# Cross attention with its scores made twice, and the experts' work placed in the next batches' steps

## The reference

```python
# cross attention: channels are attended, 8 heads of 32 tokens each; keys and values are the context
qk = einsum('bhdq,bhdl->bhql', qh, kh) / sqrt(32)      # q: x, k = v: ctx, 512 x 512 per head
ret = einsum('bhql,bhdl->bhdq', softmax(qk), vh)
x = layernorm(x + gamma * ret)
# experts: 8 of rank 16, two per token
gates = softmax(x @ Wr + br + bonus); w = two largest gates, divided by their sum
x = layernorm(x + sum_e w_e * (relu(x @ Wd_e + bd_e) @ Wu_e + bu_e))
```

## Time and profile before

| | |
|---|---|
| median of 3 runs | 2082.64 us |
| the profiled execution, its own time | 2083.66 us |
| its span (first to last instruction) | 2081.9 us |
| TensorE busy, share of the span | 1846.4 us, 89% |
| VectorE | 1249.2 us, 60% |
| ScalarE | 920.4 us, 44% |
| GpSimd | 288.0 us, 14% |
| mean granted TensorE clock | 0.952 |

### The profile page before, as it was taken

How to read it: one execution, slowest core, us unless ns; L and a number is a source line. 1 busy time by engine, 2 the same in 40 slices (tenths; PEclk the granted TensorE clock), 3 DMA queues, 4 the chain that set the end, 5 groups by cost and what they waited for, 6 DMA issues and landing times. The chain is left out here.

```text
span 2081.9 us, 33021 instructions
## 1 busy us (share of the span) xinstructions
PE 1846.4 (89%) x12272; PEld 1503.4 (72%) x12272; DVE 1249.2 (60%) x2330; ACT 920.4 (44%) x2376; POOL 288.0 (14%) x347
## 2 busy tenths in 40 slices
PE   6979999999976799999999996799997498889966
PEld 5868999998964588888888985677775365555543
DVE  3446444444434565546555536788887288878847
ACT  2224333333323343333333223666666288878811
POOL 0000000000002111111111001333343111121001
PEclk9989999999997799999999998999998699999988
DMA  3122000000013231111101013000010675556234
GB/s 104 45 97 72 21 21 21 21 21 21 10 48 101 66 97 47 36 31 41 46 19 34 11 41 121 11 31 32 31 42 21 182 179 136 153 140 149 68 114 142
DMA packets 86253, 136.62 MB, mean 66 GB/s; under 512 B 9480, under 2 KB 25480, under 8 KB 86096
## 3 DMA queue, kind: packets, MB, share of 16 engines
q1 hardware_dynamic: 86096, 134.52, 22.3%
HBM read 79.88 MB, written 21.05 MB: 48 GB/s over the span
## 5 line engine op out<-in xcount | busy, mean ns | idle before, releaser
L1164 PE MATMUL yp<-ccy,toep 128*128 128x288 f32 x640 | 182.4, 436 | 19.5 <-POOL ccy L892 13.4
L1965 ACT ACTIVATE e_p<-e_s_ps,e_nb 128x512 f32<-128x512 f32 x256 | 175.0, 696 | 51.6 <-DVE e_nb L2013 49.5
L2013 DVE TENSOR_REDUCE e_nb<-e_s_ps 128x2 f32<-128x1024 f32 x128 | 155.8, 1218 | 54.3 <-PE e_s_ps L2090 53.5
L1442 ACT ACTIVATE p<-p,nb,rq 128x128 f32<-128x128 f32 (+1 forms) x256 | 137.0, 541 | 94.5 <-DVE nb L1539 94.5
L2100 PE MATMUL e_t_ps<-ident,e_p 128*128 128x128 f32 x1024 | 148.7, 284 | 24.7 <-DVE e_pT L2020 13.2
L1164 PEld LDWEIGHTS yp<-ccy,toep 128*128 128x128 f32 x640 | 126.5, 206 | 55.7 <-POOL ccy L892 14.8
L2100 PEld LDWEIGHTS e_t_ps<-ident,e_p 128*128 128x128 f32 x1024 | 120.8, 146 | 62.5 <-issue 52.9
L80 PE MATMUL q_ps<-a_xt_hi,wq_hi 128*128 128x256 f32 x512 | 151.7, 296 | 4.1 <-DVE wo_lo L112 4.1
L1062 DVE SCALAR_TENSOR_TENSOR hm<-gu_ps,us_col,sg 128x256 f32<-128x256 f32 x88 | 42.3, 481 | 182.3 <-ACT sg L971 182.3
L82 PE MATMUL q_ps<-a_xt_hi,wq_lo 128*128 128x256 f32 x512 | 146.5, 286 | 0.0
L81 PE MATMUL q_ps<-a_xt_lo,wq_hi 128*128 128x256 f32 x512 | 146.4, 286 | 0.0
(11 more groups left out here) (277 smaller groups left out, 5122.1 us busy)
## 6 DMA issues: line engine op xcount, KB each, us to landing
x_after<-n_r SPq DMA_DIRECT2D x24, 512.0 KB, 3.0
toep<-padded_kernels SPq DMA_DIRECT2D x32, 256.0 KB, 3.5
qs<-e_xh SPq DMA_DIRECT2D x64, 128.0 KB, 2.5
qs<-e_xl SPq DMA_DIRECT2D x64, 128.0 KB, 2.6
ks<-e_ch SPq DMA_DIRECT2D x64, 128.0 KB, 2.6
ks<-e_cl SPq DMA_DIRECT2D x64, 128.0 KB, 2.6
x<-x_after SPq DMA_DIRECT2D x12, 512.0 KB, 4.7
x<-in_x SPq DMA_DIRECT2D x8, 512.0 KB, 4.1
```

The lines of the kernel that those rows point to most:

```text
L1164: last = pe.matmul(yp[:, lo % 2, 0:NCOL], toep[h % 2][:, (lo - li) * P:(lo - li + 1) * P], ccy[h % 2][:, li, 0:NCOL], start=(li == 0), sto ...
L1442: act.activation(p[n % 3][:, h, part[t]], p[n % 3][:, h, part[t]], ACT.Exp, bias=nb[i][:, t, h:h + 1], scale=rq[u][:, t:t + 1], accum_out= ...
L1965: act.activation(pr[i][:, a, :], s_ps[i][:, a, :], ACT.Exp, bias=nb[i][:, a:a + 1], accum_out=sums[t][:, j, q:q + 1]).then_inc(e_done, 1)
L2013: dve.tensor_reduce(nb[i][:], s_ps[i][:], AX.X, ALU.max, negate=True).then_inc(nb_done, 1)
```

## The change

One function, `l1_cross_and_experts`, takes the place of both.

- **Scores twice.** "Rough" scores (`rough_scores`) are one matmul of 32 rows per head and query block, from the rounded high parts alone, two heads at once in different rows of the array. They are made for the maxima only, and run 11 steps ahead (`LEAD`). VectorE writes the negated maxima (`maxima`, still 128x1024 per step) into `nbx`; a transposition (`turn_largest`, four tiles, twice a batch) and a ScalarE copy turn them into rows; four DMAs issued by ScalarE (`place_largest`) put them into row 96 of `qs`, whose partner row of `ks` holds ones. The exact scores (`scores`) have keys on partitions and 97 rows: three stacked parts and the maximum. So ScalarE's exponentials go from PSUM straight to `pT`, with no bias and no sum, and the transpositions and their copies fall away. SyncE stacks with 24 DMAs per batch in place of 32.
- **Sums.** `values` has four more matmuls that multiply by `ones`, so the sums lie in `d_ps` spread over partitions already. `normalise` takes the reciprocal of all 128x512 of them, and scales. `v_ps` and `d_ps` are single: the first values of a tile wait for the `normalise` of the tile before (`o_scaled`). GpSimd adds the residual.
- **Experts.** Their operations stand in the cross attention's steps of the next two batches, at fixed steps of each engine's order. x stays on chip; the experts' loads of x and the store and reload of the tensor between are gone.
- **PSUM.** Rough scores, context, turned maxima, x, hidden, turned and out all share `a_ps`, two slots of two banks each, strictly in turn. `take` makes TensorE wait until the reader of the use before last is done.

The diff, cut to its core (`+` and `-` where the line is new or gone; indices as in the order of the steps):

```diff
-STEPS = HX * NQ // 2
-HALF = STEPS // 2
-
-
-def l1_cross(core, ahead, after, x, ctx_in, y, gamma):
+STEPS = T * NQ * HT // 2
+UNITS = 2 * STEPS
+LEAD = 11
+NPT = 12
+KX = 3 * CX + 1
...
+def l1_cross_and_experts(core, ahead, x, ctx_in, y, gamma, wr, br, wdn, bd, wup, bu):
...
+        nbx = [sb(f"e_nbx{i}", [P, NQ, P]) for i in range(2)]
+        nbr = [sb(f"e_nbr{i}", [P, D], F32R) for i in range(2)]
+        pT = [sb(f"e_pT{i}", [P, D]) for i in range(NPT)]
+        ones = sb("e_ones", [P, CX])
+        rec = sb("e_rec", [P, D])
+        rb = [sb(f"e_rb{i}", [P, D]) for i in range(2)]
...
+        a_ps = [pb(f"e_a_ps{i}", [P, 2, D]) for i in range(2)]
+        s_ps = [pb(f"e_s_ps{i}", [P, D]) for i in range(2)]
+        v_ps, d_ps = pb("e_v_ps", [P, D]), pb("e_d_ps", [P, D])
...
+        def slot_uses(b, step, g):
+
+            if step == 1 and 0 <= b - 2 < B:
+                yield "out", b - 2
+            if step == 3 and 0 < b + 1 < B:
+                yield "context", b + 1
+            if step in (5, 13) and 0 <= 2 * b + 1 + step // 8 < 2 * B:
+                yield "largest", 2 * b + 1 + step // 8
+            if step == 8 and 0 <= b - 1 < B:
+                yield "x", b - 1
+            if step == 10 and 0 <= b - 1 < B:
+                yield "hidden", b - 1
+            if step == 15 and 0 <= b - 1 < B:
+                yield "turned", b - 1
+            if 0 <= g + LEAD < PAIRS_IN_ALL:
+                yield "pair", g + LEAD
+
+        place = {("context", 0): 0}
+        for at in steps():
+            for use in slot_uses(*at):
+                place[use] = len(place)
...
+                for b, step, g in steps():
+                    if step == 3 and 0 <= b - 2 < B:
+                        power(b - 2, mv6, mv6_done, y6_done, rstd6, ve6_done, rstd6_done)
+                    if step == 3 and 0 <= b - 1 < B:
+                        residual(b - 1, 1)
+                    if step == 6 and 0 <= b - 1 < B:
+                        power(b - 1, mv5, mv5_done, y5_done, rstd5, ve5_done, rstd5_done)
+                    if step == 6 and b + 2 < B:
+                        scale_x(b + 2)
+                    if step == 10 and b + 2 < B:
+                        take_lo(pool, b + 2, "cl")
+                    if step == 11 and 0 <= b < B:
+                        residual(b, 0)
+                    if step == 12 and b + 2 < B:
+                        take_lo(pool, b + 2, "xl")
...
+                def place_largest(n):
+
+                    b, t = divmod(n, T)
+                    act.wait_ge(nbr_done, n + 1)
+                    if b >= 2:
+                        act.wait_ge(s_mm, UNITS * (b - 2) + UNITS // 2 * (t + 1))
+                    for j in range(HT):
+                        act.dma_start(qs[b % 2][KX - 1:KX, t, j, :].bitcast(F32),
+                                      nbr[n % 2][j * CX:j * CX + 1, :].bitcast(F32)).then_inc(biased, 16)
+
+                def exps(u):
+                    act.wait_ge(s_mm, u + 1)
+                    if u >= NPT:
+                        act.wait_ge(pv_mm, (u - NPT) // HT + 1)
+                    act.activation(pT[u % NPT][:], s_ps[u % 2][:], ACT.Exp).then_inc(e_done, 1)
...
+                for b, step, g in steps():
+                    if step == 1 and 0 <= b - 2 < B:
+                        hidden(b - 2)
+                    if step in (6, 14) and 0 <= 2 * b + 1 + step // 8 < 2 * B:
+                        place_largest(2 * b + 1 + step // 8)
+                    if 0 <= g < PAIRS_IN_ALL:
+                        exps(2 * g)
+                        exps(2 * g + 1)
+                    if step == 4 and 0 < b + 1 < B:
+                        context(b + 1)
+                    if step in (5, 13) and 0 <= 2 * b + 1 + step // 8 < 2 * B:
+                        round_largest(2 * b + 1 + step // 8)
+                    if step == 9 and 0 <= b - 1 < B:
+                        turned(b - 1)
+                    if step == 9 and b + 2 < B:
+                        round_hi(b + 2, "ch")
+                    if step == 11 and b + 2 < B:
+                        round_hi(b + 2, "xh")
+                    if step == 12 and 0 <= b - 1 < B:
+                        exponential(b - 1)
...
+                def maxima(n):
+                    b, t, q, jj = pair(n)
+                    half = n // (STEPS // 2)
+                    dve.wait_ge(a_mm, n + 1)
+                    if half >= 2:
+                        dve.wait_ge(n_turned, half - 1)
+                    heads = nbx[half % 2][:, q, :].rearrange("p (j c) -> p j c", c=CX)[:, 2 * jj:2 * jj + 2, 0]
+                    dve.tensor_reduce(heads, slot("pair", n)[:], AX.X, ALU.max, negate=True).then_inc(nb_done, 1)
+
+                def normalise(n):
+                    dve.wait_ge(pv_mm, NQ * (n + 1))
+                    if n:
+                        dve.wait_ge(o_scaled, n)
+                    dve.reciprocal(rec[:], d_ps[:]).then_inc(rec_done, 1)
+                    dve.wait_ge(rec_done, n + 1)
+                    if n >= 2:
+                        dve.wait_ge(added5, n - 1)
+                    dve.scalar_tensor_tensor(rb[n % 2][:], v_ps[:], gcol[:, 0:1], rec[:], ALU.mult, ALU.mult)\
+                       .then_inc(o_scaled, 1)
...
+                def add_experts(b):
+                    dve.wait_ge(o_mm, b + 1)
+                    dve.tensor_tensor(rr[b % 2][:], slot("out", b)[:], rr[b % 2][:], ALU.add).then_inc(added6, 1)
...
+                for u in range(2):
+                    dve.memset(ks[u][KX - 1:KX, :, :, :].bitcast(F32), 1.0).then_inc(set_up, 1)
+                take_lo(dve, 0, "cl")
+                take_lo(dve, 0, "xl")
+                dve.wait_ge(set_up, 5)
+                dve.wait_ge(g_loaded, 16)
+                for b, step, g in steps():
+                    if step == 2 and 0 <= b - 2 < B:
+                        add_experts(b - 2)
+                    if step == 11 and 0 <= b - 1 < B:
+                        shift(b - 1)
+                    if 0 <= g + LEAD < PAIRS_IN_ALL:
+                        maxima(g + LEAD)
+                    if b == 0 and step == 0:
+                        dve.wait_ge(w_loaded, 64)
+                        dve.tensor_scalar(bias[:, 0, 0:E], bias[:, 0, 0:E], BONUS, None, ALU.add).then_inc(prepared, 1)
+                        dve.wait_ge(prepared, 3)
+                    if step in (2, 10) and 0 <= 2 * b - 1 + step // 8 < 2 * B:
+                        normalise(2 * b - 1 + step // 8)
+                    if step == 2 and 0 <= b - 2 < B:
+                        statistics(b - 2, added6, b - 1, st6, st6_done, mv6, mv6_done)
+                    if step == 4 and 0 <= b - 2 < B:
+                        apply(b - 2, mv6, rstd6, rstd6_done, y6_done)
+                    if step == 5 and 0 <= b - 1 < B:
+                        statistics(b - 1, added5, T * b, st5, st5_done, mv5, mv5_done)
+                    if step == 7 and 0 <= b - 1 < B:
+                        apply(b - 1, mv5, rstd5, rstd5_done, y5_done)
+                    if step == 13 and 0 <= b - 1 < B:
+                        gate(b - 1)
+                        choose(b - 1)
+                    if step == 14 and 0 <= b - 1 < B:
+                        picks(b - 1)
+                        weigh(b - 1)
 
...
+                def take(kind, n, *freed):
+
+                    i = place[kind, n] % 2
+                    if read[i]:
+                        pe.wait_ge(*read[i])
+                    read[i] = freed
+                    return a_ps[i]
...
+                def rough_scores(n):
+
+                    b, t, q, jj = pair(n)
+                    if t == q == jj == 0:
+                        pe.wait_ge(xh_done, b + 1)
+                        pe.wait_ge(ch_done, b + 1)
+                    bank = take("pair", n, nb_done, n + 1)
+                    for i in range(2):
+                        j = 2 * jj + i
+                        d = slice(j * CX, (j + 1) * CX)
+                        last = pe.matmul(bank[:, i, :], xh[b % 2][d, t, q * P:(q + 1) * P], ch[b % 2][d, t, :],
+                                         start=True, stop=True, skip_group_check=True, tile_position=(j * CX, 0))
+                    last.then_inc(a_mm, 1)
+
+                def turn_largest(n):
+                    pe.wait_ge(nb_done, STEPS // 2 * (n + 1))
+                    bank = take("largest", n, nbr_done, n + 1)
+                    for q in range(NQ):
+                        last = pe.transpose(bank[:, 0, q * P:(q + 1) * P], nbx[n % 2][:, q, :], core.ident[:])
+                    last.then_inc(n_turned, 1)
+
+                def scores(u):
+                    b, t, k, j = unit(u)
+                    if k == 0:
+                        pe.wait_ge(stacked[j], 16 * 6 * (b + 1))
+                        pe.wait_ge(biased, 16 * HT * (T * b + t + 1))
+                    if u >= 2:
+                        pe.wait_ge(e_done, u - 1)
```

(39 more changed lines are left out.)

652 lines of the change are left out of this document (224 added, 428 removed).

## The result

The kernel after takes **2296.49 us** (median of 4 runs, 2294.99 to 2297.78); the kernel before, run beside it, 2086.91. The ratio is 1.100, with a 95% interval of 1.097 to 1.104. The forecast was 2195, with a range of 2100 to 2240: slower, as said, but by 210 us where 112 were forecast.

A forecast was written before the change was run, and what follows sets the result against it. The prediction took three engines in step, with their order deciding. Start and batch 0 to 1709, then 54.5 + 310 + 51 + 40.5 gave 2165; 29 for the clock made a span of 2194, time 2195 us, range 2100 to 2240.

The forecast's parts named there:

- What bounds the kernel: Late cross-attention batches of 40 us: no engine has much room, and TensorE, VectorE and ScalarE go in step.
- The walk: Engine orders followed through a middle batch: waits for slots, readers and scaling make it 62 us where it took 40.
- the clock term of the sum: Two TensorE idle times of 4.8 us per batch cost some 2 us each: 66 per batch, 29 in all.
- The start: From 1629.8 us: first exponentials near 1660, router's weights about 1669, 40 for the rest of batch 0, ending at 1709.
- TensorE's sum: TensorE's work in a batch after the change: 37 us, as much as before, in a form that waits.
- faster: Rival for the batches: the slots' waits hide, 42 us per batch, 2027 us in all; chance 0.14.
- The tail: Behind batch 7: a bare chain from two normalisations through the experts to the store, 40.5 us.
- Cheap and dear reciprocals: Rivals in normalise: 0.63 us each, 2133 us, chance 0.17; or 4.5 to 7.8 us, 2217 to 2270, chance 0.05.
- Rough pairs one after the other: Rival for TensorE's rough scores: 0.57 us a pair, at most 3.5 more per batch, 25 in all; no chance given.
- what would show it: Profile signs: reciprocals some 3 us, two idle times over 3, TensorE well under 75% busy, clock below 0.9, tail 40.
- the rough pairs mostly start without a wait: Sign in TensorE's profile that would show the prediction wrong; no size given.

The follow-up runs named there:

- e13: The kernel of e12 with half of its filling multiplications in TensorE's waits: 2196.7 us.
- e5: The changed kernel with one DMA in place of four for the maxima of a tile: 2238.9 us.
- e12: The kernel of e5 with small multiplications, results unread, in every TensorE wait of more than 1 us: 2287.9 us.
- e14: e10 with shift read between the second reciprocal's halves, and unread multiplications ahead of first pairs, first scores and in the tail: 2062.8 us.
- e7: e5 with normalise, norm and routing earlier, and ScalarE's and VectorE's reads of shared slots ahead of their steps' long work: 2087.1 us.
- e10: e9 with each reciprocal in two halves, step 9's maxima between the second one's halves, first values of a tile one step later: 2081.3 us.
- e1: The changed kernel with twelve unread score matmuls ahead of the values of steps 3 and 11: 2259.5 us.
- e9: e7 with GpSimd setting the ones, ScalarE issuing half the first stacking, router's weights loaded first, last batch's norm earlier: 2081.1 us.

## Why the prediction was wrong, step by step

- **What bounds the kernel** was read rightly: the three engines go in step, and the order decides, not the sums.
- **The walk was right in its waits, and partly lucky in its length.** It gave 62 us per batch without its clock term. The waits stand where it put them: ahead of the values 4.3 in step 3 and 4.8 in step 11 (forecast 4.8 each), ahead of the pair 1.9 in step 4 and 1.5 in step 0. Its prices were low by small amounts: the reciprocal 3.35 for 3.1, four DMA issues 2.43 for 1.6, a rough pair 0.43 of issue for 0.35; over a batch 0.5 + 1.7 + 1.3, so 65.5. e13, with one DMA and the clock nearly full, has 62 to 65. The luck: 62 us with a TensorE sum of 37 leave 25 for its idle time; measured are 43.6 of work and 20.5 idle, 64.1 together. The work was 6.6 too low and the idle time 4.5 too high.
- **The step that failed is the clock term of the sum:** "two idle times of 4.8 us per batch ... should cost some 2 us each: 66 us per batch". By the walk with the measured prices it came to 82 less 65.5, **over 16 us and not 4**; by TensorE's own time to 82 less 64.1, 18. Both are worked out; what runs that change little else gave back of it is 6.5 to 9.7 us per batch (e13 against e5, whose clock of 0.77 to 0.81 left less to give back). The term took its price from one idle time with nothing but dense work behind it and applied it only to the two longest waits. Even those rows say more than 2 us: of the time from 1737.77 to 1744.40, 5.9 us were at the lower level, which costs 3. Six more waits of 1.1 to 2.3 us lie in every batch, most of them steps of the walk itself; the lower level follows most of them, and from 1905 to 1925 it lasted through 20 us of nearly unbroken work. By the start of step 1, batches 2 to 6 take 82, 82, 82, 78 and 82 where 66 each were forecast; that is 76 of the 99 us by which the span was missed. The start makes 12.5, batch 1 makes 8, batch 7 with the tail 7, less the 5 set aside for the clock elsewhere.
- **TensorE's sum** of 37 us was 6.6 low (43.6 by e12). It became the bound once the waits were gone: e14's batches of 45.6 hold it and little else. So the rival "faster", 42 per batch with hidden waits and 2027 us, was out of reach by its own sum; its condition, batches under 50, was met in e7, and e7 came out even, not faster: its batches, 49.5 on average, save no more than its start and its tail cost.
- **The start** was walked rightly as far as it was walked: the first exponentials at 1657.7 (forecast 1660), the router's weights at 1666.8 (forecast 1669). But the rest of batch 0 took 54.7 us and not 40, to 1721.5 (forecast 1709): the clock was 0.55 from 1640 to 1680 and 0.71 from 1680 to 1720, and TensorE was idle for 21 of these 80 us; how much each cost was not tried.
- **The tail** took 39.4 us from the last reciprocal, 2253.8, to the end (the bare chain was forecast at 40.5); from step 1 of batch 7 to the end it was 98.7 for 91.5.
- **Cheap and dear reciprocals** both fall with 3.35. The halves of e10 take 1.76 and 1.74: 6.3 ns per element over the second 256 columns, and some 0.15 fixed. The Trainium skill ("VectorE: DVE Perf Modes", "First, the fixed hardware budget") gives a repeat count of 8, by which the prediction estimated 4.4 us; the measured 3.35 does not agree and decides.
- **Rough pairs one after the other** falls too: a pair lasts 0.50, as long as one matmul, so its two parts run side by side; the next instruction starts 0.43 behind it, inside the bounds of 0.28 and 0.57.
- Of "what would show it", the reciprocals, the two waits, the first exponentials and the tail came as told. TensorE was busy for 75% and not well under: work at half speed counts as busy, so the share looked healthier than the batch was. The clock was 0.7 in the batches where "below 0.9" was asked, and its distance from 0.9 was what mattered. One sign of being wrong was there: the rough pairs mostly start without a wait, 13 of 16 in a batch. The three that wait (1.9, 1.5 and 1.8) were enough, so the sign was badly chosen.

## What to carry to other kernels

A wait of TensorE is paid twice where it makes the clock fall, and a wait of 2 us can do that as well as one of 5, even one of 0.84 (e14), though the same wait does not always do it (e7). So sum all waits on the path, and price the work behind them at both levels. Where one slot is shared by many readers in a fixed order, put every reader ahead of the long work of its step: orders of this kind, with one DMA in place of four, were worth 210 us here, and no other operation of the change had to go. Before mending waits, add up the bounding engine's work at full clock from a run that has no waits; it tells what the mending can reach.

## What the runs showed of the hardware that was not expected

- TensorE can stay at the 1.2 GHz level while it is busy: 1905 to 1925 us, busy for 18.7 of 20, granted clock 0.50.
- Equal waits in equal places are followed by either level: 2.46 us twice in e7, 0.86 and 0.84 in e14.
- Useless matmuls in the waits make a kernel faster: e1 by 37 us, e13 by 42 against e5; twice as many, which outlast the waits, make it 49 slower (e12 against e5).
- While SyncE and ScalarE both issue stacking DMAs, an issue takes mostly some 1.3 us on each (e9), where SyncE alone takes 0.60 to 0.70 in e7: the 24 take 14.3 us together and 16.5 on SyncE alone, so a second queue gains little.
- An fp32 multiplication of 128 columns is two recorded instructions of 0.115 us each at full clock (e12), where a transposition of the same size is one.
